# Layer norm in the first stage's last round: the order of mean and variance on TensorE

## The chip, the cores and the metric

One core of one Trainium2 chip runs the whole program. The metric is the device time of one launch in microseconds (us), the median of three runs. Engines are TensorE (PE; its weight loads are PEld), VectorE (DVE), ScalarE (ACT), GpSimd (POOL) and SyncE (SP).

## The reference, cut to what matters

Two layers act on x (8 batches, 256 tokens, 256 channels). The first layer is an LSTM, linear attention, an RNN and a 16-expert feed-forward. The second layer begins with another LSTM, whose output is normalized before its attention projects it:

```python
def _L1_attn_ref(x, Wq, bq, Wk, bk, Wv, bv, gamma, beta):
    mu = jnp.mean(x, axis=-1, keepdims=True)
    var = jnp.mean(jnp.square(x - mu), axis=-1, keepdims=True)
    xn = (x - mu) * jax.lax.rsqrt(var + LN_EPS) * gamma + beta
    ...
```

The x of this function is the output of the second layer's LSTM (`_L1_cond_ref`), 256 tokens of 8 batches. The change touches only mu and var.

## The kernel before, in words

Three stages follow one another: `pipeline_one` (first layer, the second layer's LSTM and this layer norm), `attention_two`, and `pipeline_two`. Tokens are cut into NCH = 16 chunks of C = 16 tokens (CW = 128 columns of token and batch). `pipeline_one` runs NI = 20 rounds i of 16 slots each, and then four more slots. One slot is one time step of the LSTMs; the e-LSTM (second layer) runs LAG = 4 rounds behind the a-LSTM. Each engine has its own instruction list, written out by the loop over `steps()`, and takes it strictly in that order; semaphores tie the lists together. There is no planner: the order of the calls in the loops is the order of the work.

The ring of one LSTM step is: TensorE's `lstm_step` (L584; matmuls at L596) fills the gates in PSUM, VectorE transposes them (`gate_turn`, L1036), ScalarE takes a tanh (L840), VectorE makes the cell (L1043, L1045, L1048 in `cell`), ScalarE takes its tanh (L846), VectorE makes the new state lh (`state`, first instruction L1060), and TensorE's next `lstm_step` waits for lh.

In round 19, the last, most other work has run out, and the layer norm begins beside the ring. `UNITS` lists 9 units of tokens: seven pairs of chunks (units 0 to 6, 256 columns) and two single chunks (units 7 and 8). `UNIT_AT` gives unit 0 to round 18's slot 15, units 1 to 6 to round 19's slots 0 to 5, and unit 7 to slot 7; unit 8 comes behind the loop. For unit u in its slot:

- TensorE, at the end of its slot: `norm_mean(u)` (L766, matmuls at L775), two fp32 matmuls in four records, with the unit's columns moving, into PSUM bank xy[0]. It waits for the centering of unit u-1 (`n_d`), which read that bank.
- VectorE, between `cell` and `state`: `norm_center(u)` (L1260, instruction L1263) waits for `n_mean` and subtracts the mean in place.
- ScalarE, at the end of its slot: `norm_square(u)` (L953, instruction L958) into one of two buffers, sq[u % 2], over tmp and gs.
- TensorE, one slot later: `norm_var(u)` (L779, matmuls at L787) waits for `n_sq` and makes four fp32 matmuls of one moving column, with the squares as 128x128 weights, in eight records, into bank xy[1].

Where a slot has both a `norm_var` (of unit u-1) and a `norm_mean` (of unit u), TensorE's list has them at L825 to L828, behind all its other work of the slot. That is so in slots 0 to 5 of round 19. In slot 15 of round 18 and in slot 7 there is only a mean, in slots 6 and 8 only a variance. The first root over the variances (`norm_sqrt(0)`, L960) is taken in slot 7 and wants units 0 to 6. Slots 3 and 6 also have an LSTM input projection (L453), slot 1 a product into z (L105).

Of the kernel before, what the change touches and what calls it, by code (L numbers as in the profile page):

```python
# [64 lines left out]
def attends(i):  # L65

    return 1 <= i <= NCH
# [32 lines left out]
def split_matmul(pe, out, w, x, start, last=False):  # L100

    ins = None
    for k in range(KT):
        for wp, xp in ((0, 0), (1, 0), (0, 1)):
            ins = pe.matmul(out, w[wp](k), x[xp](k), start=start, stop=last and k == KT - 1 and xp == 1,  # L105
                            skip_group_check=True)
            start = False
    return ins


def pipeline_one(nc, t, xs, hs1, x2d, late, qkv):


    with ExitStack() as ctx:
# [138 lines left out]
        def wh(n, m):  # L253

            return (lambda k: w_hi[n][:, k, m * P:(m + 1) * P], lambda k: w_lo[n][:, k, m * P:(m + 1) * P])

        def cols(hi, lo, a, b):
            return (lambda k: hi[:, k, a:b], lambda k: lo[:, k, a:b])

        def bias(n, m):  # L260
            o = NB[n][0] + m * P
            return brow[:, o:o + P]
# [198 lines left out]
        def project_c(pe):  # L461

            for m in range(KT):
                pe.matmul(g_c[:, :, m, :], bias("c_b", m), ones2[:, :], start=(m == 0), stop=False,
                          skip_group_check=True)
                last = split_matmul(pe, g_c[:, :, m, :], wh("c_wx", m), cols(x1_h, x1_l, 0, CW), False)
            return last
# [9 lines left out]
        def steps():  # L477

            return [(i, slot) for i in range(NI + 1) for slot in range(C if i < NI else E0)]

        def xn(c, n):

            return hs1[:, :, (LAG + 1 + c) * CW:(LAG + 1 + c + n) * CW]
# [15 lines left out]
        def unit_at(i, slot, lag):  # L499

            return UNIT_AT.get(i * C + slot - lag)

        def pair_at(i, slot, lag):

            return PAIR_AT.get(i * C + slot - lag)
# [77 lines left out]
        def _(pe):  # L583
            def lstm_step(i, slot):  # L584

                n = i * C + slot
                par, u = slot // QS % 2, slot % QS
                on = [(0, "a_wh")] * (i < NCH) + [(1, "e_wh")] * (n >= FIRST_STEP["e"])
                pe.wait_ge(l_hi, n)
                for w, part in ((w_hi, 0), (w_lo, 0), (w_hi, 1)):  # L590
                    if part == 1:
                        pe.wait_ge(l_lo, n)
                    for ae, name in on:
                        for k in range(KT):
                            for j in range(4):
                                last = pe.matmul(gate_block(ae, j, par), lh[:, part, ae, k, u, :],  # L596
                                                 columns(w[name], k, j), start=False, stop=(part == 1 and k == KT - 1),
                                                 skip_group_check=True, tile_position=(0, j * 32))
                last.then_inc(l_pe, 1)
# [18 lines left out]
            def rnn_step(i, slot):  # L618
                n = nth("c", i, slot, NCH * C)
                if n is None:  # L620
                    return
                s = n % C
                prev = (s - 1) % C * B
                pe.wait_ge(c_hi, n)
                pe.wait_ge(c_32, n)
                for m in range(KT):
                    for k in range(KT):
                        for wt in (w_hi, w_lo):
                            pe.matmul(g_c[:, s, m, :], wt["c_wh"][:, k, m * P:(m + 1) * P],
                                      c_hh[:, k, prev:prev + B], start=False, stop=False, skip_group_check=True)  # L630
                pe.wait_ge(c_lo, n)
                for m in range(KT):
                    for k in range(KT):
                        last = pe.matmul(g_c[:, s, m, :], w_hi["c_wh"][:, k, m * P:(m + 1) * P],
                                         c_hl[:, k, prev:prev + B], start=False, stop=(k == KT - 1),
                                         skip_group_check=True)
                last.then_inc(c_pe, 1)
# [62 lines left out]
            def w1(i, slot):  # L700

                n = nth("w1", i, slot, N_E)
                if n is None:
                    return
                for h in range(2):
                    if n > 0:
                        pe.wait_ge(g_32, 2 * n - 1 + h)
                    pe.matmul(xy[h][:, :], w1s[:, n % E1, :],
                              tst[:, n // E1 % 2, 4 * h:4 * h + 4, :].rearrange("p h n -> p (h n)"), start=True,
                              stop=True).then_inc(xy_full, 1)  # L710

            def spread(i, slot):

                n = nth("w2", i, slot, N_E)
                if n is None:
                    return
                pe.wait_ge(z_free, Z_AT[n // E1 + 2, 14] + 1)
                pe.wait_ge(gp_free, n)
                if slot == 2 and attends(i):
                    pe.wait_ge(v_read, i)  # L720
                if slot in (5, 7) and attends(i):
                    pe.wait_ge(nd_read, 2 * (i - 1) + (slot - 3) // 2)
                for k in range(KT):
                    for wt in (wt_h, wt_l):
                        last = pe.matmul(gp[:, k, :], sel[:, n % E1, k, :], wt[:, :], start=(k == 0 and wt is wt_h),
                                         stop=(wt is wt_l), skip_group_check=True)
                last.then_inc(gp_full, 1)

            def values(i, slot):

                if i > 1:
                    pe.wait_ge(nd_read, 2 * (i - 1))
                split_matmul(pe, gp[:, KT:2 * KT, :].rearrange("p k n -> p (k n)"),
                             (lambda k: ac_h[:, k, :], lambda k: ac_l[:, k, :]),
                             (lambda k: w_hi["wv"][:, k, :], lambda k: w_lo["wv"][:, k, :]), start=True,
                             last=True).then_inc(v_full, 1)
# [29 lines left out]
            def norm_mean(u):  # L766

                c, n = UNITS[u]
                pe.wait_ge(e_kept, 2 * (c + n))
                pe.wait_ge(g_32, 2 * N_E)  # L770
                pe.wait_ge(prep_set, 3)
                if u > 0:
                    pe.wait_ge(n_d, u)
                for k in range(KT):
                    last = pe.matmul(xy[0][:, 0:n * CW], mean_w[:, :], xn(c, n)[:, k, :], start=(k == 0),  # L775
                                     stop=(k == KT - 1))
                last.then_inc(n_mean, 1)
# [23 lines left out]
            for i, slot in steps():  # L801
                if (i, slot) == (LAG, E0):
                    pe.wait_ge(e_reset, 2)
                if (i, slot) == (1, 0):
                    pe.wait_ge(rest_lo, LO_MAIN)
                    pe.wait_ge(loaded_const, 16 * (len(consts) + 1))
                    pe.wait_ge(row2_sent, 16)
                elif (i, slot) == (LAG, 0):
                    pe.wait_ge(rest_lo, LO_ALL)
                lstm_step(i, slot)  # L810
                w1(i, slot)
                rnn_step(i, slot)
                misc(i, slot)
                spread(i, slot)
                if slot == 1 and attends(i):
                    values(i, slot)
                project_steps(i, slot)
                if slot in (4, 6) and attends(i):
                    sums(i, slot // 2 - 2)
                w2(i, slot)  # L820
                if slot == C0 - 1 and attends(i):
                    pe.wait_ge(x1_split, i)
                    pe.wait_ge(c_32, (i - 1) * C)
                    project_c(pe)
                if unit_at(i, slot, 1) is not None:  # L825
                    norm_var(unit_at(i, slot, 1))
                if unit_at(i, slot, 0) is not None:
                    norm_mean(unit_at(i, slot, 0))  # L828
                if pair_at(i, slot, 0) is not None:
                    norm_spread(pair_at(i, slot, 0))  # L830
            norm_mean(NPAIR)
# [1567 lines left out]
```

## Time and profile before

| | |
|---|---|
| median of 3 runs (lowest to highest) | 2730.02 us (2724.48 to 2731.41) |
| profiled execution, its own time | 2729.23 us |
| its span, first to last instruction | 2727.2 us |
| PE busy / PEld busy | 2445.4 us (90%) / 2042.8 us (75%) |
| DVE busy / ACT busy / POOL busy | 1926.5 us (71%) / 1156.3 us (42%) / 398.2 us (15%) |
| mean granted TensorE clock | 0.94 of full speed |

Busy shares are means over three stages with different limits. Times in a timeline are counted from the first instruction. A "granted clock" of 1.00 is TensorE's 2.4 GHz, 0.50 is 1.2 GHz. A matmul's end is modelled; its start and the starts and ends on DVE and ACT are recorded.

### The profile page before, as it was taken

What the parts mean: (1) busy time and instruction counts of PE and PEld (TensorE: products, weight loads), DVE (VectorE), ACT (ScalarE), POOL (GpSimd) and SP (SyncE); (2) the same over time, 40 slices, a digit from 0 to 9 for tenths busy, and PEclk for the clock granted to TensorE, in tenths of its full rate; (3) what the DMA queues carried; (4) which work ended last, traced back from release to release, by engine and by line L of the source; (5) the groups of instructions that cost most, each with busy time, mean ns of one, the idle gap of its engine ahead of it and who ended that gap; (6) DMA issues with size and microseconds to landing.
All of it is one profiled execution on the core that took longest, in us unless ns stands there. A gap on an engine that the chain in (4) does not pass through costs nothing. (4 is left out here: it accounts for less than half of the span.)

```text
span 2727.2 us, 119354 instructions
## 1 busy us (share of the span) xinstructions
PE 2445.4 (90%) x50848; PEld 2042.8 (75%) x50848; DVE 1926.5 (71%) x7414; ACT 1156.3 (42%) x3693; POOL 398.2 (15%) x412
## 2 busy tenths in 40 slices
PE   3678999999999999987768859999999999999999
PEld 1455677777777777654536648999999999999998
DVE  4757777777777777788666656677777776666774
ACT  3225555555555555556346722333333333333333
POOL 0000000000000000000019701222222222222222
PEclk9668999999999999999859958999999999999999
DMA  5000000000000000100013230000000000000000
GB/s 171 1 2 3 5 5 6 5 5 5 5 5 5 5 5 5 36 12 27 4 44 108 77 109 7 9 9 9 9 9 9 9 9 9 9 9 9 5 5 6
DMA packets 53051, 53.66 MB, mean 20 GB/s; under 512 B 24982, under 2 KB 47144, under 8 KB 50602
## 3 DMA queue, kind: packets, MB, share of 16 engines
q1 hardware_dynamic: 47318, 29.70, 4.0%
q0 software_dynamic: 1728, 12.58, 1.3%
q8 instruction: 402, 6.59, 1.0%
q10 hardware_dynamic: 3476, 3.75, 0.5%
q14 instruction: 127, 1.04, 0.1%
HBM read 39.46 MB, written 6.55 MB: 17 GB/s over the span
## 5 line engine op out<-in xcount | busy, mean ns | idle before, releaser
L105 PE MATMUL p<-xn,m_h 128*128 128x128 f16 x6144 | 559.1, 220 | 0.0
L105 PE MATMUL p<-xn,m_l 128*128 128x128 f16 x3072 | 530.3, 220 | 0.0
L105 PEld LDWEIGHTS p<-xn,m_h 128*128 128x128 f16 x6144 | 480.9, 98 | 1.8
L596 PE MATMUL lg_b<-xn,lh 128*32 128x256 f16 x6144 | 303.0, 294 | 85.5 <-DVE lh L1060 77.3
L2119 POOL TENSOR_TENSOR xn<-qkv_w,xn 128x384 f16<-128x384 f32 x256 | 234.3, 915 | 904.5 <-ACT xn L2077 904.5
L1036 DVE STREAM_TRANSPOSE gt<-lg_b 128x512 f32<-128x512 f32 x324 | 230.2, 710 | 187.1 <-PE lg_b L596 184.8
L840 ACT ACTIVATE gl<-gt 128x128 f32<-128x128 f32 x324 | 100.2, 309 | 602.8 <-DVE gt L1036 602.1
L855 ACT ACTIVATE hm<-xy,b 128x512 f32<-128x512 f32 x512 | 347.9, 680 | 0.0
L105 PEld LDWEIGHTS p<-xn,m_l 128*128 128x128 f16 x3072 | 301.1, 98 | 0.7
L2003 PE MATMUL po<-m_h,xn 128*128 128x256 f16 x1536 | 292.6, 272 | 1.9 <-DVE xn L2158 1.9
L596 PEld LDWEIGHTS lg_b<-xn,lh 128*32 128x32 f16 x6144 | 161.1, 102 | 173.3 <-DVE lh L1060 128.8
L596 PE MATMUL lg_b<-e_wh_hi,lh 128*32 128x256 f16 x4096 | 210.8, 283 | 31.3 <-DVE lh L1060 29.1
L2067 ACT ACTIVATE cand<-g_b 128x16 f32<-128x16 f32 x256 | 47.1, 184 | 385.2 <-PE g_b L1967 385.2
L2003 PE MATMUL po<-m_l,xn 128*128 128x256 f16 x768 | 208.8, 272 | 0.0
L2233 DVE SCALAR_TENSOR_TENSOR zm<-zr,cand 128x16 f32<-128x16 f32 x256 | 44.4, 173 | 204.2 <-ACT cand L2067 202.1
L762 PE MATMUL yo<-hm,w2f 128*32 128x256 f32 x2048 | 162.3, 390 | 25.1 <-DVE tmp L1086 24.8
L2077 ACT ACTIVATE xn<-qkv_w 128x384 f16<-128x384 f32 x256 | 133.9, 523 | 106.1 <-DVE qkv_w L2142 106.1
L2062 ACT ACTIVATE zr<-g_b 128x32 f32<-128x32 f32 x256 | 50.6, 198 | 270.4 <-PE g_b L1951 270.4
L1945 PEld LDWEIGHTS g_b<-xn,gxu_w 128*128 128x128 f16 x4096 | 136.5, 96 | 38.1 <-DVE xn L2238 33.1
L2227 DVE TENSOR_TENSOR rh_l<-rh,rh_h 128x16 f16<-128x16 f32 x256 | 143.5, 561 | 27.7 <-DVE rh L2223 1.4
L2003 PEld LDWEIGHTS po<-m_h,xn 128*128 128x128 f16 x1536 | 148.8, 97 | 17.5 <-issue 2.3
L1945 PE MATMUL g_b<-xn,gxu_w 128*128 128x8 f16 x4096 | 140.5, 166 | 23.0 <-DVE xn L2238 21.9
(387 smaller groups left out, 6218.2 us busy)
## 6 DMA issues: line engine op xcount, KB each, us to landing
m_stage<-in_m_w POOLq DMA_DIRECT2D x12, 1024.0 KB, 5.2
hs<-in_m_w SPq DMA_DIRECT2D x14, 384.0 KB, 3.2
x_dram<-x SPq DMA_DIRECT2D x16, 128.0 KB, 2.1
xs<-in_l_wv SPq DMA_DIRECT2D x1, 2048.0 KB
attention_dram<-att SPq DMA_DIRECT2D x16, 128.0 KB, 2.8
xn<-x_dram SPq DMA_DIRECT2D x16, 128.0 KB, 2.4
out_dram<-xn SPq DMA_DIRECT2D x16, 128.0 KB, 2.2
xn<-attention_dram SPq DMA_DIRECT2D x124, 16.0 KB, 1.7
```

The costliest lines, as they stand in the source:

```text
L105: ins = pe.matmul(out, w[wp](k), x[xp](k), start=start, stop=last and k == KT - 1 and xp == 1, skip_group_check=True)
L596: last = pe.matmul(gate_block(ae, j, par), lh[:, part, ae, k, u, :], columns(w[name], k, j), start=False, stop=(part == 1 and k == KT - 1) ...
L762: last = pe.matmul(yo[q * HD:(q + 1) * HD, :, :], w2f[:, n % E1, :], tok[:, :, q, :], start=True, stop=True, skip_group_check=True, tile_p ...
L840: act.activation(gl[:, :].rearrange("p (m b) -> p m b", b=B), gt[:, :].rearrange("p (m n) -> p m n", n=32)[:, :, slot % QS * B:(slot % QS ...
L855: act.activation(hm32[:, n % 2, h * 512:(h + 1) * 512], xy[h][:, :], ACT.Gelu, bias=b1[:, n % E1:n % E1 + 1], scale=1.0 / S).then_inc(g_32, 1)
L1036: dve.transpose(gt[:, :], lg_b[slot // QS % 2][:, :, :, :].rearrange("p g a x -> p (g a x)"))\
L1945: pe.matmul(o[:, slot % 8, m, :], w[:, k, m * P:(m + 1) * P], h(g_hh, k), start=False, stop=False, skip_group_check=True)
L2003: last = pe.matmul(po[:, half, :], x[:, n % 2, r], w[:, tl, :], start=(first and x is a_h and w is m3_h), stop=(end and x is a_l), skip_gr ...
L2062: act.activation(zr[:, :], g_b[slot // 8][:, slot % 8, 0:4].rearrange("p m b -> p (m b)"), ACT.Tanh, scale=0.5 / S).then_inc(zr_act, 1)
L2077: act.activation(a_h[:, n % 2, :], a32[:, n % 2, :], ACT.Copy).then_inc(a_hi, 1)
L2119: pool.tensor_tensor(a_l[:, n % 2, :], a32[:, n % 2, :], a_h[:, n % 2, :], ALU.subtract).then_inc(a_lo, 1)
L2227: dve.tensor_tensor(rh_l[:, :, :], rh32[:, :].rearrange(kb, b=B), rh_h[:, :, :], ALU.subtract).then_inc(rh_lo, 1)
```

## The change

In TensorE's loop `norm_mean` of a slot's unit is put ahead of `norm_var` of the unit before. No instruction is added or removed, no wait is changed, and the other engines' lists stay as they are.

```diff
@@ -822,10 +822,10 @@
                     pe.wait_ge(x1_split, i)
                     pe.wait_ge(c_32, (i - 1) * C)
                     project_c(pe)
+                if unit_at(i, slot, 0) is not None:
+                    norm_mean(unit_at(i, slot, 0))
                 if unit_at(i, slot, 1) is not None:
                     norm_var(unit_at(i, slot, 1))
-                if unit_at(i, slot, 0) is not None:
-                    norm_mean(unit_at(i, slot, 0))
                 if pair_at(i, slot, 0) is not None:
                     norm_spread(pair_at(i, slot, 0))
             norm_mean(NPAIR)
```

## Rows read from the trace of the kernel before

**Rows 1.** The page: busy time by engine, and the granted clock in 40 slices.
```profile
PE 2445.4 (90%) x50848; PEld 2042.8 (75%) x50848; DVE 1926.5 (71%) x7414; ACT 1156.3 (42%) x3693; POOL 398.2 (15%) x412
PEclk9668999999999999999859958999999999999999
```
**Rows 2.** Busy by windows: length, PE, PEld, DVE, ACT, POOL, clock, DMA, GB/s.
```profile
1302.00:1415.00 113.00, 73.99 (x934) 46.31 (x927) 72.61 (x256) 41.33 (x101) 1.17 (x4) 0.67 0.01 3
1415.00:1700.00 285.00, 229.28 (x3649) 193.42 (x3648) 173.47 (x484) 142.30 (x449) 133.87 (x68) 0.81 0.29 82
```
**Rows 3.** Waits from 1315.3 to 1347.5: total us, times, longest.
```profile
DVE hs L1263 <- PE xy L775: 6.3, 5, 2.2
```
**Rows 4.** Timeline, slot 1 of round 19: start, duration, engine, line.
```profile
1325.03 0.72 DVE L1036 STREAM_TRANSPOSE gt<-lg_b 128x512 f32<-128x512 f32 x1 [1.18 <-PE lg_b L596]
...
1326.27 1.02 PEld L787 LDWEIGHTS xy<-mean_w,gs 128*128 128x128 f32 x8
...
1326.45 0.19 DVE L1048 SCALAR_TENSOR_TENSOR cl<-pl_ 128x32 f32<-128x32 f32 x1
...
1327.24 1.11 PE L775 MATMUL xy<-hs,mean_w 128*128 128x256 f32 x4
1328.38 0.69 DVE L1263 TENSOR_TENSOR hs<-hs,xy 128x512 f32<-128x512 f32 x1 [1.74 <-PE xy L775]
1328.99 0.18 DVE L1060 SCALAR_TENSOR_TENSOR lh<-gl,tl_ 128x32 f16<-128x32 f32 x1
...
1329.23 0.12 PEld L596 LDWEIGHTS lg_b<-e_wh_hi,lh 128*32 128x32 f16 x8 [1.28 <-DVE lh L1060]
```
**Rows 5.** Timeline, slot 0.
```profile
1319.15 1.48 PEld L787 LDWEIGHTS xy<-mean_w,tmp 128*128 128x128 f32 x8 [0.21 <-issue]
...
1320.57 2.05 PE L775 MATMUL xy<-hs,mean_w 128*128 128x256 f32 x4
...
1322.66 0.69 DVE L1263 TENSOR_TENSOR hs<-hs,xy 128x512 f32<-128x512 f32 x1 [1.72 <-PE xy L775]
```
**Rows 6.** Timeline, slot 2.
```profile
1330.91 1.11 PE L775 MATMUL xy<-hs,mean_w 128*128 128x256 f32 x4
...
1332.03 0.19 DVE L1048 SCALAR_TENSOR_TENSOR cl<-pl_ 128x32 f32<-128x32 f32 x1
1332.14 0.68 DVE L1263 TENSOR_TENSOR hs<-hs,xy 128x512 f32<-128x512 f32 x1
```
**Rows 7.** Timeline, slots 3 and 4.
```profile
1338.19 0.69 DVE L1263 TENSOR_TENSOR hs<-hs,xy 128x512 f32<-128x512 f32 x1 [2.23 <-PE xy L775]
...
1339.03 0.12 PEld L596 LDWEIGHTS lg_b<-e_wh_hi,lh 128*32 128x32 f16 x8 [1.28 <-DVE lh L1060]
...
1339.93 0.72 DVE L1036 STREAM_TRANSPOSE gt<-lg_b 128x512 f32<-128x512 f32 x1 [0.51 <-PE lg_b L596]
...
1341.36 0.19 DVE L1048 SCALAR_TENSOR_TENSOR cl<-pl_ 128x32 f32<-128x32 f32 x1
...
1341.88 0.69 DVE L1263 TENSOR_TENSOR hs<-hs,xy 128x512 f32<-128x512 f32 x1 [0.33 <-PE xy L775]
```
**Rows 8.** Timeline, slot 6, where there is a variance and no mean.
```profile
1348.92 1.78 PEld L787 LDWEIGHTS xy<-mean_w,tmp 128*128 128x128 f32 x8 [0.41 <-issue]
...
1349.45 0.19 DVE L1060 SCALAR_TENSOR_TENSOR lh<-gl,tl_ 128x32 f16<-128x32 f32 x1 [0.29 <-ACT tl_ L846]
...
1350.72 0.14 PEld L596 LDWEIGHTS lg_b<-e_wh_hi,lh 128*32 128x32 f16 x8
...
1352.24 0.72 DVE L1036 STREAM_TRANSPOSE gt<-lg_b 128x512 f32<-128x512 f32 x1 [2.20 <-PE lg_b L596]
```
**Rows 9.** Windows between the changes of clock.
```profile
1319.90:1326.00 6.10, 5.22 (x43) 3.69 (x44) 2.43 (x9) 1.39 (x4) 0.00 (x0) 0.50 0.01 3
...
1336.80:1347.20 10.40, 7.75 (x104) 5.70 (x107) 5.70 (x20) 2.97 (x7) 0.24 (x1) 0.98 0.00 0
1347.80:1367.00 19.20, 14.67 (x168) 9.42 (x160) 11.14 (x44) 7.48 (x17) 0.00 (x0) 0.50 0.01 2
```

## The prediction

> **What bounds the kernel now.** I read the page first: TensorE is busy for 90% of the span, at a clock that is full but for the start and the slices around the middle [rows 1]. That share says nothing of the place that the change touches, so I cut the span by stages. The stretch from 1302 to 1415 us is the end of the first stage: of 113 us TensorE is busy for 74.0, VectorE for 72.6, and the mean clock is 0.67 [rows 2]. Nobody is full there; it is a ring of latencies. Everything behind it starts when it ends, so a microsecond taken out of the ring is one off the span, and one taken elsewhere is none.
>
> Then the list of waits for the slots concerned (slot 15 of round 18 to slot 5 of round 19). VectorE's centering, L1263, stood idle for TensorE's mean, L775, five times and 6.3 us in all [rows 3]. This wait is on the ring: the centering stands in VectorE's list ahead of the new state lh, and TensorE's next step needs lh. The timeline of slot 1 shows the chain [rows 4]. TensorE starts the variance's weight loads at 1326.27, the mean's matmuls only at 1327.24, and they end at 1328.35. VectorE had issued the cell at 1326.45 and had then nothing to do until 1328.38. The centering is followed by lh 0.61 us later (1328.99), and by TensorE's next step at 1329.23. So from the mean's end to the next step there are 0.88 us (1329.23 - 1328.35) in which TensorE idles, and in front of the mean stand 0.97 us of variance (1327.24 - 1326.27) that nobody on the ring wants.
>
> **What the change does.** Its count is zero: nothing is added, nothing removed; six times, in slots 0 to 5, eight load and matmul records of a variance go behind the four of a mean. No DMA and no other queue is passed. Two waits are moved with them. The mean's wait, for the centering of the unit before, was met a slot ago. The variance's wait, for the square of the unit before, now stands behind the mean, which makes it less often late. What is queued behind the variance is TensorE's next LSTM step.
>
> The gain per slot has three caps. First, it can't be more than VectorE's wait. Second, it can't be more than the variance that goes out of the way: 0.97 us at 2.4 GHz, and 1.42 us in slot 0 (1319.15 to 1320.57), where the clock fell on the way [rows 4, 5]. Third, the variance now lies between the mean and the next step, in the 0.88 us that centering and state take. TensorE must finish it before it takes the next step; what it ran over came off the gain. Where TensorE's queue decides, the slot goes from variance + mean + 0.88 to mean + variance: the gain is 0.88 whatever the clock is, as long as VectorE was waiting for at least that long.
>
> Slot by slot:
> - Slot 0, wait 1.72 us [rows 5]: 0.88. The next step would start right behind the variance; VectorE, which has its cell by then, is no longer last.
> - Slot 1, wait 1.74 [rows 4]: 0.88. The mean's end comes 0.97 earlier, and the variance then runs for 0.97 in a cover of 0.88, so TensorE is last by 0.09.
> - Slot 2: the mean ends at 1332.02 and the cell starts at 1332.03, so the centering at 1332.14 waited for nothing [rows 6]: 0. The order can't hurt either: TensorE is finished at the same time as before, 0.96 us ahead of where the next step may start.
> - Slot 3, wait 2.23 [rows 7]: 0.88. Here the projection is in front of both, and over 0.9 us of the wait stays.
> - Slot 4, wait 0.33 [rows 7]: VectorE's own order decides then. In slot 2 the centering starts 0.11 us behind the start of the cell (1332.03 to 1332.14) [rows 6]; here it would start at 1341.47 in place of 1341.88: 0.41.
> - Slot 5 repeats slot 4 with the same wait of 0.33, the fifth of the five in [rows 3]: 0.41.
>
> The sum is 3 x 0.88 + 2 x 0.41 = 3.46 us. The cost of moving the variance is nothing where the centering covers it. If that cover were gone it would be its 0.97 us at full clock and 1.8 at 1.2 GHz: slot 6 shows a variance that really is in the way, with lh begun at 1349.45 and the next step at 1350.72, only when its loads end [rows 8]. The same rows bound what the trace doesn't show, the hand-over from a mean to a variance and from a variance to a step: the step's load began 0.02 us behind the variance's last load (1350.70 to 1350.72), so I take it as nothing. Worst it is the 0.41 us which a first load idled behind other work in slot 6, three times in the three queue-bound slots, 1.2 us; best, loads slip under the mean's last matmul and the three slots give the whole 0.97, 0.3 us more. The sum thus lies between 2.2 and 3.8.
>
> Nothing later waits for the variance sooner: the root over units 0 to 6 is in slot 7, behind the variance of slot 6, which isn't moved. So the profiled execution would go from 2729.23 to 2725.8 us. It lies 0.8 us under the median of the three runs, so on that scale the forecast is 2726.6.
>
> **The clock.** It is the one thing that the change may move by more than its own sum. It stood at 1.2 GHz from 1319.9 to 1326.0, at 2.4 through slots 4 and 5, and at 1.2 again from 1347.8 to 1367 [rows 9]. TensorE had its idle gap in each of the full slots and kept the clock for 10.4 us with 7.75 busy. The change takes idle time out of five slots and no work.
>
> The Trainium skill (TensorE: Matmul & The Clock Gate, section "Why this matters for your kernels") asks for dense work with no idle gaps to hold the higher level. By that rule the change also buys clock, which is the second case below; this trace is only half on its side, since the clock that held in 10.4 us with 7.75 busy was gone behind them [rows 9].
>
> **The rivals.**
> - The clock holds into slots 6 to 8. Those are at 1.2 GHz now. A step from its first load to the transpose takes 1.52 us there (1350.72 to 1352.24) and 0.90 at full clock (1339.03 to 1339.93) [rows 7, 8]: 0.62 for each of three slots, and in slot 6 the variance would end before lh and free another 1.03 (1350.72 less 1349.69, which is lh's start plus the 0.24 from lh to a step). That is 2.9 us, so 2723.7. For it: less idling. Against it: that fall came right behind slots 4 and 5, in which the change saves only 0.41 us of idling each.
> - The other side: the clock falls earlier, so that slots 4 and 5, full now, run at half. Then a step costs 0.62 more, and mean and variance together take 3.6 us in place of 1.8 (twice slot 6's 1.8, one for each as they are about alike) from 0.1 us ahead of the transpose. The next step starts 3.5 behind the transpose, where by VectorE alone it would be 2.4 (1.54 to the centering, 0.61 and 0.24). Each slot loses 0.6 + 1.1 = 1.7. Two such slots and half a one in slot 3 lose 4.3, against 3.5 won: slower by 0.8, so 2730.8. It decides from two lost slots on. For it: the clock was down twice here [rows 9] beside waits of at most 2.2 us [rows 3]. Against it: no pause gets longer.
> - The change does nothing: the hand-overs between fp32 loads eat what the mean wins, the wait on the mean becomes one on TensorE's queue, and the next step starts where it did. 2730.0. Against it is the 0.02 us of slot 6; for it, only that no slot of before has a variance behind a mean.
>
> **How the numbers follow.** The forecast, 2726.6, gets 0.62, the held clock 0.15, the earlier fall 0.12, nothing 0.11. A measurement of this kernel can tell about 0.3% from no change, 8.2 us; every case lies within that. What is left is the scatter: three runs of the same kernel lie 7 us apart, and the attention stage runs at a mean clock of 0.81 over 285 us [rows 2], which a shift may disturb either way. The range takes the cases from 2723.7 to 2730.8 and 3 to 5 us beyond: 2719 to 2734. Faster by over 0.3% (under 2721.8) I give 0.09, mostly from the held clock; slower by as much 0.03; within 0.3% 0.88.
>
> **What would show it.** In slots 0 to 5 the mean's matmuls start where the variance's loads did. L1263's wait for L775 falls from 6.3 us to about 2 (0.8 left in slot 1, some 1.2 in slot 3, near none in 0, 4 and 5). Slots 4 and 5 last 0.41 us less from transpose to transpose. In slots 0 and 1 TensorE's next step starts right behind the variance's last load, without the 0.88 of idling. The first stage ends some 3.5 us earlier, and nothing before slot 0 moves. The prediction is wrong if that wait stays at 6 us, if the slots don't shorten where it falls, or if the changes of clock move and carry more than the wait.

## The result and the profile after

The changed kernel takes 2716.51 us (median of 8 runs, 2714.97 to 2722.57) against 2725.39 (8 runs, 2721.86 to 2731.88): a ratio of 0.9962, with a 95% interval of 0.9949 to 0.9975. That is 8.9 us in place of the forecast 3.4 (2730.02 less 2726.6), and 2716.51 lies below the range. On another chip it was 2718.07 against 2730.41, ratio 0.9951 [0.9935, 0.9966]; one run of before there took 7198.22 us and is left out of all medians and ranges here. The profiled execution takes 2716.23 us, its span 2714.4.

The page of the changed kernel, answering to [rows 1]: TensorE's busy time falls by 12.6 us without one instruction less. The same matmuls ran at a higher clock, but only 4.2 us of this fall lie in the slots that the change touches; 7.6 lie ahead of them and 0.9 behind.
```profile
PE 2432.8 (90%) x50848; PEld 2038.1 (75%) x50848; DVE 1925.9 (71%) x7414; ACT 1154.7 (43%) x3693; POOL 397.5 (15%) x412
PEclk9678999999999999999869859999999999999999
```
The waits of the same slots (1309.3 to 1336.4 here), answering to [rows 3]:
```profile
DVE hs L1263 <- PE xy L775: 1.6, 3, 1.3
```
The wait that was to go has gone from 6.3 to 1.6 us, near the 2 that was expected, though not where: 1.26 are left in slot 1 and 0.20 in slot 3, where 0.8 and 1.2 were expected. Slot 1's timeline, answering to [rows 4]:
```profile
1318.01 0.72 DVE L1036 STREAM_TRANSPOSE gt<-lg_b 128x512 f32<-128x512 f32 x1 [1.72 <-PE lg_b L596]
...
1319.36 1.48 PE L775 MATMUL xy<-hs,mean_w 128*128 128x256 f32 x4
1319.43 0.19 DVE L1048 SCALAR_TENSOR_TENSOR cl<-pl_ 128x32 f32<-128x32 f32 x1
...
1320.46 1.08 PEld L787 LDWEIGHTS xy<-mean_w,gs 128*128 128x128 f32 x8
...
1320.88 0.69 DVE L1263 TENSOR_TENSOR hs<-hs,xy 128x512 f32<-128x512 f32 x1 [1.26 <-PE xy L775]
1321.48 0.18 DVE L1060 SCALAR_TENSOR_TENSOR lh<-gl,tl_ 128x32 f16<-128x32 f32 x1
...
1321.72 0.12 PEld L596 LDWEIGHTS lg_b<-e_wh_hi,lh 128*32 128x32 f16 x8 [0.18 <-DVE lh L1060]
```
The mean comes first, and the variance's eight loads (1320.46, 1.08 us) lie where TensorE had idled; the next step's load waits 0.18 us for lh in place of 1.28. The prediction had TensorE last here by 0.09 us, and it isn't. Slot 0, answering to [rows 5], shows the other case: at 1.2 GHz the variance ends behind lh, and the step's load (1316.49) starts only when the variance's loads end (1314.43 + 2.04).
```profile
1314.43 2.04 PEld L787 LDWEIGHTS xy<-mean_w,tmp 128*128 128x128 f32 x8
...
1315.10 0.69 DVE L1263 TENSOR_TENSOR hs<-hs,xy 128x512 f32<-128x512 f32 x1 [0.16 <-PE xy L775]
1315.70 0.18 DVE L1060 SCALAR_TENSOR_TENSOR lh<-gl,tl_ 128x32 f16<-128x32 f32 x1
...
1316.49 0.14 PEld L596 LDWEIGHTS lg_b<-e_wh_hi,lh 128*32 128x32 f16 x8
```
Slots 3 and 4, answering to [rows 7]: 0.20 us of slot 3's 2.23 are left, and slot 4's centering starts 0.10 us behind the cell.
```profile
1328.17 0.69 DVE L1263 TENSOR_TENSOR hs<-hs,xy 128x512 f32<-128x512 f32 x1 [0.20 <-PE xy L775]
...
1329.92 0.72 DVE L1036 STREAM_TRANSPOSE gt<-lg_b 128x512 f32<-128x512 f32 x1 [0.51 <-PE lg_b L596]
...
1331.34 0.19 DVE L1048 SCALAR_TENSOR_TENSOR cl<-pl_ 128x32 f32<-128x32 f32 x1
1331.44 0.68 DVE L1263 TENSOR_TENSOR hs<-hs,xy 128x512 f32<-128x512 f32 x1
```
**Where the 12.8 us between the two profiled executions went.** I measured each profile by VectorE's transposes, one per LSTM step, in three parts: up to the transpose of round 18's slot 15; the "stretch" of eight steps from there to round 19's slot 7, which holds every slot that the change touches; and what lies behind. The first part (1315.56 and 1309.55 us) is 6.0 us shorter in the changed kernel, though no instruction in it differs. The stretch takes 36.68 and 29.92 us, 6.8 less. The rest is equal within 0.1. The stretch's own row for the changed kernel (length, PE, PEld, DVE, ACT, POOL, clock, DMA, GB/s):
```profile
1309.55:1339.47 29.92, 25.37 (x347) 20.73 (x348) 19.68 (x70) 8.72 (x23) 0.58 (x2) 0.89 0.02 7
```
Its mean clock is 0.89; in the kernel before it was 0.79 by the same view. So three questions were open: whether the 6.0 us ahead belong to the change, what the order is worth at one clock, and what moved the clock.

### The profile page after: what moved, and what is told of

Its sections match the earlier page's. It is cut to its first block and busy times, and to the rows that moved or that the text cites. A ratio compares the mean times of both kernels' runs of the same rounds, so it can differ in the third digit from the quotient of the medians.

```text
span 2714.4 us, 119354 instructions
## 1 busy us (share of the span) xinstructions
PE 2432.8 (90%) x50848; PEld 2038.1 (75%) x50848; DVE 1925.9 (71%) x7414; ACT 1154.7 (43%) x3693; POOL 397.5 (15%) x412
```

## The experiments

Each row has one profile, which shows the clock in one execution. "Stretch" is as above; "low" is the time in it at 1.2 GHz. Ratios are against the kernel before on the same chip; its medians on the five other chips were 2727.9 to 2730.4 us.

| kernel | median us (lowest to highest, runs) | ratio [95%] | stretch | low |
|---|---|---|---|---|
| before, first profile | 2725.39 (2721.86 to 2731.88, 8) | | 36.68 | 15.7 |
| b_null: before again | 2729.55 (2720.43 to 2734.72, 12) | 0.9991 [0.9978, 1.0004] | 46.34 | 41.0 |
| b_p1: before again | 2729.01 (1) | | 43.06 | 32.2 |
| b_p2: before again | 2722.02 (1) | | 36.68 | 15.7 |
| after, first profile | 2716.51 (2714.97 to 2722.57, 8) | 0.9962 [0.9949, 0.9975] | 29.92 | 6.8 |
| a_again: changed again | 2718.07 (2714.57 to 2719.13, 6) | 0.9951 [0.9935, 0.9966] | 27.42 | 0 |
| a_p1: changed again | 2716.22 (1) | | 29.92 | 6.8 |
| a_again2: changed again | 2716.96 (2713.78 to 2718.48, 6) | 0.9962 [0.9948, 0.9977] | 27.40 | 0 |
| b_fill: before, 2 extra matmuls a slot | 2718.88 (2715.37 to 2721.55, 6) | 0.9955 [0.9939, 0.9971] | 30.40 | 0 |
| b_fill1: before, 1 extra a slot | 2718.40 (2717.60 to 2722.32, 10) | 0.9968 [0.9958, 0.9977] | 30.39 | 0 |
| a_fill: changed, 2 extra a slot | 2717.53 (2714.60 to 2719.91, 6) | 0.9954 [0.9938, 0.9969] | 27.70 | 0 |
| b_filltail: before, extra to stage end | 2718.09 (2714.67 to 2721.80, 12) | 0.9962 [0.9950, 0.9975] | 30.40 | 0 |
| a_filltail: changed, extra to stage end | 2717.44 (2714.80 to 2721.07, 12) | 0.9957 [0.9945, 0.9969] | 27.69 | 0 |
| s01: swapped in slots 0, 1 | 2724.28 (2716.20 to 2733.37, 12) | 0.9988 [0.9970, 1.0006] | 29.15 | 0 |
| s345: swapped in slots 3, 4, 5 | 2718.73 (2716.53 to 2724.86, 12) | 0.9967 [0.9953, 0.9980] | 36.89 | 20.5 |
| s12345: swapped in slots 1 to 5 | 2720.72 (2716.21 to 2721.28, 6) | 0.9964 [0.9951, 0.9976] | 30.53 | 6.8 |
| b_fill15: before, 4 extra in slot 15 | 2726.18 (2718.42 to 2737.01, 12) | 0.9990 [0.9975, 1.0004] | 46.40 | 41.4 |
| a_idle: changed, VectorE delay | 2717.99 (2715.34 to 2724.59, 10) | 0.9964 [0.9948, 0.9980] | 29.43 | 0 |
| a_novar2: changed, variances left out (output wrong) | 2715.65 (2714.11 to 2720.33, 6) | 0.9961 [0.9946, 0.9976] | 27.40 | 0 |
| b_split: half of each variance ahead | 2715.97 (2710.40 to 2732.45, 12) | 0.9960 [0.9947, 0.9974] | 42.20 | 38.2 |

**1. Both kernels again, and both with the clock held up.** The edit of b_fill and a_fill puts matmuls with unused results at the end of TensorE's work in slot 15 and slots 0 to 6, in the order of before and in the changed one:
```diff
+            def fill(k):
+                if k not in FILL:                # FILL = {k: 2 for k in range(8)}
+                    return
+                pe.wait_ge(gp_free, N_E)
+                for _ in range(FILL[k]):
+                    pe.matmul(gp[:, :, :].rearrange("p k n -> p (k n)"), w_hi["c_wh"][:, 0, 0:P],
+                              w_hi["c_wx"][:, :, :].rearrange("p k n -> p (k n)"), start=True, stop=True, ...)
...
                     norm_spread(pair_at(i, slot, 0))
+                fill(i * C + slot - NORM)
```


> The kernel before once more, unchanged. It measures the scatter and gives a second look at where the clock falls. Theory A (the order's own gain is 3 to 3.5 us, and the rest of the difference is TensorE clock: part of it brought by the order, part by chance in places the change doesn't touch): no difference beyond 0.15% (4 us) in the medians, but the times of the first mean in the two profiles may differ by some us. From the transpose of round 18's slot 15 to that of round 19's slot 7 it takes 36.7 us in the profile of before; another profile may show 33 to 37, by where the clock falls. Rival B (the whole difference comes from the order alone and each profile repeats): 36.7 within 0.3, and the first mean within 1 us of 1315.4.

> The changed kernel once more. Theory A: 6 to 10 us under before by the medians; from slot 15's transpose to slot 7's 28 to 32 us (29.9 in the first profile), with slots 4 and 5 again 0.41 shorter each than before. Rival B: the same 29.9 within 0.3, and the first mean 6 us earlier than in every profile of before, which would say that something ahead of the changed slots has changed.

> The order of before, with two extra fp16 matmuls (128x128 weights, 512 columns, results unused, about 0.43 us at full clock) behind TensorE's work of slot 15 and slots 0 to 6 of the last rounds; they fit into the 0.88 us in which TensorE idled there. Theory A (the clock falls for TensorE's idling): the clock stays up through these slots, and from slot 15's transpose to slot 7's it takes 31 to 33 us in place of 36.7, so about 4 us faster than before without the change of order. Rival B (clock has nothing to do with it): within 0.5 us of before, or slower by up to 3 us as the extra matmuls stand in the way.

> The changed order with the same extra matmuls. Theory A: the stretch from slot 15's transpose to slot 7's takes 28 to 29.5 us, 3 to 3.5 less than the same extra matmuls in the order of before: the order's own gain at one clock. About 1 us faster than the changed kernel, as its one low stretch of 6.9 us at slot 0 goes too. Rival B: the difference between the two orders with the extra matmuls is the same 6.8 us as without them, and this kernel is no faster than the changed one.

Measured: the kernel before gives the same median, but its second profile is quite another: the stretch takes 46.34 us, nearly all of it at 1.2 GHz.
```profile
1309.84:1356.18 46.34, 39.35 (x347) 28.27 (x348) 20.03 (x71) 8.73 (x23) 0.58 (x2) 0.56 0.01 4
```
Its slot 15 transpose is at 1309.84, against 1315.56 in the first profile and 1309.55 in the changed kernel. So the 6 us ahead of the stretch are chance. Over all four profiles of each kernel the mean of that time is 1310.8 and 1310.9; the means of the stretch are 40.7 and 28.7. The stretch carries the whole difference.

The changed kernel again, with no low clock in the stretch:
```profile
1312.74:1340.16 27.42, 22.23 (x347) 18.13 (x348) 19.59 (x71) 8.73 (x23) 0.59 (x2) 1.00 0.02 7
```
With extra matmuls in the order of before, and then in the changed order:
```profile
1310.70:1341.10 30.40, 26.35 (x363) 18.60 (x364) 19.86 (x71) 8.72 (x23) 0.58 (x2) 1.00 0.02 6
```
```profile
1309.21:1336.91 27.70, 25.69 (x363) 18.80 (x364) 19.58 (x70) 8.71 (x23) 0.58 (x2) 1.00 0.02 7
```
This is the main finding. More work on TensorE made the kernel before 11.5 us faster (2718.88 against 2730.41), with its order untouched. In its profile the clock stayed at 2.4 GHz, and the stretch is 10.3 us under the mean of before. And at one clock the two orders lie 2.70 us apart. The extra matmuls cost the changed order 0.28 (27.70 against 27.42), so its own gain is 3.0. Theory A held in kind, but its sizes were off. It looked for 33 to 37 us in b_null (46.34), 28 to 32 in a_again (27.42), 31 to 33 and 4 us gained in b_fill (30.40 and 11.5), and 28 to 29.5 in a_fill (27.70), which is no faster than the changed kernel beyond the scatter.

**2. The swap in part of the slots, and extra matmuls to the end of the stage.** The swap is bound to `i == NI - 1 and slot in (0, 1)`, or `(3, 4, 5)`. In the other two FILL runs on with five a slot, three where there is a spread matmul.

> The mean goes ahead of the variance in slots 0 and 1 alone. With extra matmuls in both orders the order's own gain at full clock was 2.70 us (30.40 less 27.70 from slot 15's transpose to slot 7's), of which slots 0 and 1 had 0.36 and 0.90. Theory A1 (the clock is lost or kept by the idling around slots 15, 0 and 1, and a low stretch begun there feeds on itself): 1.3 us of the order's own, and most of the 7 to 9 us of clock: 8 to 10 us under before. Theory A2 (every slot's idling adds its share to the chance of a fall): 1.3 plus about a third of the clock: 3 to 5 us under before, and slots 3 to 6 are still found at the low clock in the profile or in the scatter of the times, which stays at 10 us or more.

> The mean goes ahead of the variance in slots 3, 4 and 5 alone; the order's own gain there at full clock was 0.62, 0.41 and 0.42, 1.45 us. Theory A1: the low stretch of slots 0 and 1 stays and may run on: 1.5 to 4 us under before. Theory A2: 1.5 plus half of the clock or more: 5 to 7 us under before.

> The order of before with extra matmuls (results unused) to the end of the first stage: two a slot up to round 19's slot 6, then five a slot, three where the slot has a spread matmul. In every profile so far the clock is low for some 50 us behind slot 6 or 7 and the 12 steps behind slot 7's transpose take 49.9 us. Theory A (the idling brings the low clock): these 12 steps take 43 to 46 us, and the kernel is 15 to 19 us under before. Rival (the extra matmuls hold up the steps, or the clock falls for another reason): 49 us or more, 9 to 12 us under before as with the extra matmuls in the first slots alone.

> The changed order with the same extra matmuls to the end of the stage. Theory A: 2.7 us less than the order of before with them from slot 15's transpose to slot 7's, and 2 to 3.5 us less by the medians: what the order is worth when the clock is taken out. The fastest kernel of this study, 17 to 21 us under before. Rival (the order's whole effect was the clock): the two with extra matmuls are within 1 us.

Measured: A1 fails. The swap in slots 0 and 1 left the times spread from 2716 to 2733 us, and its interval reaches 1; that in slots 3 to 5 gave 9.5 us though its profile has a low stretch of 20.5 us from slot 0 on. That low stretch ended in slot 3, the first swapped one (the clock is back 25.2 us behind slot 15's transpose), where the order of before stayed low into slot 6 in two of four profiles. A2 fits s01 (3 to 5 us under before was 3.9, with a scatter of 17) and is too small for s345 (5 to 7 was 9.5).
```profile
1312.59:1349.48 36.89, 30.84 (x347) 22.99 (x348) 19.88 (x71) 8.73 (x23) 0.58 (x2) 0.72 0.02 5
```
The profiles at full clock throughout also size the order slot by slot, from transpose to transpose: slot 0 3.61 (b_fill1) to 3.25, slot 1 4.91 to 4.02, slot 2 3.25 both, slot 3 4.45 (s01) to 3.55, slot 4 3.68 to 3.26, slot 5 3.67 to 3.26. That is 0.36 + 0.89 + 0 + 0.90 + 0.42 + 0.41 = 2.98 us.

Behind slot 7 the extra matmuls did not pay: the 12 steps took 51.84 and 50.01 us where they take 48.7 to 49.95 in all others, and neither kernel came to the 15 to 21 us under before that theory A gave them (10.1 and 10.8). The clock was up for longer parts, but the matmuls stood in front of steps, as the rival had it. The two orders differ by 2.71 us in the stretch; the medians by 0.65, which a scatter of 6 us can't tell from either.

**3. The idling put back, and more profiles.** a_idle adds one product to VectorE's part of slots 0 to 5:
```diff
+                if i == NI - 1 and slot < 6:
+                    dve.tensor_tensor(dmx[:, :, :], rcd[:, :, :], att[:, :, :], ALU.mult)
                 if slot == E0 and i > LAG:
```


> The changed order, with one extra VectorE product (128x256 fp32, result unused, about 0.4 us) between the centering and the state in slots 0 to 5: each step waits 0.4 us longer and TensorE idles as long as it did before the change. Direct cost at full clock: 6 x 0.4 = 2.4 us or less, as slots 1 and 3 are bound by TensorE's queue, so about 1.5 to 2.4. Theory A (less idling on TensorE is what keeps the clock): more than the direct cost is lost; in part of the executions the slots fall to the low clock again, the times scatter over 10 us or more as before the change, and the median is 4 to 8 us above the changed kernel. Rival C (it is the order itself, variance behind mean, that keeps the clock, whatever the idling): 1.5 to 2.4 us above the changed kernel, with its narrow scatter of 5 us.

> The kernel before, one more look at where the clock falls. So far slot 15's transpose to slot 7's took 36.7 and 46.3 us. Theory A: between 31 (clock kept throughout, which the filled order of before shows at 30.4) and 46.5 (low throughout), and not the same as both others.

> The kernel before, again one look: between 31 and 46.5 us. The mean over the four looks at this order should be 8 to 12 us above the mean of the looks at the changed order (29.9 and 27.4 so far), if this stretch alone makes the difference of the medians.

> The changed kernel, a third look: 27.4 to 31 us from slot 15's transpose to slot 7's, whatever the phase of the clock. If one look shows it low throughout (over 38 us), the change doesn't protect from the low clock and the theory of a self-sustaining low stretch falls.

Measured: the stretch is 29.43 us, 2.0 more than the changed kernel at full clock, as the direct cost was worked out. The clock stayed up in the profile and the median is that of the changed kernel; three of ten runs lie at 2721.7 to 2724.6, where one of the changed kernel's 21 is above 2720. TensorE idles for 5.0 us of slots 0 to 5, against 5.4 in the kernel before and 3.0 in the changed one at full clock. So pauses of nearly the old sum did not bring the loss back, which speaks against theory A in its plain form (less idling keeps the clock); rival C is nearer. Whether the three slower runs had a low stretch isn't shown. The other profiles came out as expected: 43.06 and 36.68 before, 29.92 changed.

**4. What in the order keeps the clock.** a_novar2 skips the variances of units 0 to 5 and fills their columns with one small matmul (`if u < 6: pe.sem_inc(n_var, 1); return`), b_split calls `norm_var` for the unit's first chunk ahead of `norm_mean` and for the second behind it. b_fill1 has `FILL = {k: 1 for k in range(8)}`.

> The changed kernel again, beside the next three. 2716 to 2719 us, with a scatter of 5 us or little more; from slot 15's transpose to slot 7's 27 to 30 us.

> The changed kernel without the variance matmuls of units 0 to 5 (their variances are a constant here, so the output is wrong): nothing stands between the mean and the next step, at either clock. Theory D (what keeps a low stretch going is idling at the low clock; in the changed order a variance of 1.8 us at 1.2 GHz covers the 0.88 us in which VectorE works, so TensorE doesn't idle there and the clock comes back; in the order of before it idles 0.88 us in every slot at any clock): taking this work away brings the idling back. The kernel is not faster than the changed one, though it has 48 matmul records less: 0 to 5 us slower, with a scatter of 8 us or more, and low slots of about 4.4 us in the profile where a full one takes 3.3. Rival E (less work on TensorE's queue is simply faster, the clock follows chance): 0.5 to 1.5 us faster than the changed kernel, with its scatter.

> Half of each variance (the unit's first chunk) stays ahead of the mean, half goes behind it, in slots 0 to 5. At full clock the centering then waits 0.47 us less in slots 0, 1 and 3 and 0.33 to 0.41 less in 4 and 5; at 1.2 GHz the half behind the mean takes 0.9 us and covers the 0.88. Theory D: no idling at the low clock, so low stretches end as in the changed kernel: 6 to 10 us under before, within 2 us of the changed kernel, scatter 5 to 8 us. Rival E: half of the order's own gain, 1 to 2 us under before, with the scatter of before.

> The order of before with one extra matmul a slot in place of two (about 0.2 us at full clock, 0.43 at 1.2 GHz; result unused), slot 15 to slot 6. It leaves some 0.45 us idle per slot at the low clock where two left nearly none. Theory D: in between, 3 to 9 us under before, and low stretches of several slots are still met in some executions, so a scatter of 8 us or more. Rival E: within 1 us of before.

Measured: theory D falls at both ends. With the variances left out there is nothing to cover VectorE's 0.88 us, and no low clock came in its profile; the stretch takes exactly as long as with them.
```profile
1311.32:1338.72 27.40, 17.65 (x301) 12.21 (x302) 19.57 (x71) 8.73 (x23) 0.58 (x2) 1.00 0.02 7
```
Rival E wanted 0.5 to 1.5 us off and got 1.3 in the median, none of it from the stretch. That also shows that the variance behind the mean costs nothing at full clock. With the variances split, most runs are fast (ten of twelve at 2710 to 2720 us), but two took 2730 and 2732, a scatter of 22 us where theory D gave 5 to 8, and the profile of the slowest has the clock low for 38 of 42 us:
```profile
1313.09:1355.29 42.20, 39.09 (x347) 30.40 (x347) 20.02 (x71) 8.72 (x23) 0.58 (x2) 0.55 0.02 5
```
In its low slots TensorE is hardly ever idle; this is slot 4 (its L1066 is L1060 of before, the new state):
```profile
1340.05 1.01 PE L787 MATMUL xy<-mean_w,tmp 128*128 128x1 f32 x4
...
1340.92 2.05 PE L775 MATMUL xy<-hs,mean_w 128*128 128x256 f32 x4
...
1342.77 0.85 PE L787 MATMUL xy<-mean_w,tmp 128*128 128x1 f32 x4
...
1343.86 0.62 PE L596 MATMUL lg_b<-e_wh_hi,lh 128*32 128x256 f16 x8 [0.24 <-DVE lh L1066]
```
Its idle time is 0.24 us of 5.2, and the clock stayed low all the same. One extra matmul a slot did about as much as two: 2718.40 us with a scatter of 4.7, where theory D wanted 8 or more and rival E no gain.

**5. Where the low clock starts.** s12345 keeps the variance first in slot 0 alone; b_fill15 has `FILL = {0: 4}`.

> The mean goes ahead of the variance in slots 1 to 5, and not in slot 0. In the profiles so far the clock fell 3.7 to 4.7 us behind slot 15's transpose in all six kernels with the variance first in slot 0, in two of seven with the mean first there, and in none of five with extra matmuls in slot 15. Theory F (the fall is decided in slots 15 and 0, by TensorE's pause in slot 15 and what stands first in slot 0; how long the low stretch lasts is decided by the order in the slots behind): the profile has the fall 4 us behind slot 15's transpose, and the median lies 2 to 4 us above the changed kernel's, 6 to 9 us under before. Rival G (the slots behind decide alone): within 1 us of the changed kernel.

> The order of before, with four extra matmuls in slot 15 alone (0.9 us in the 1.7 us pause behind the mean of unit 0, results unused). Theory F: no fall in slot 0 in the profile; slots 3 to 5 can still fall, as with the mean ahead in slots 0 and 1 alone (2724.3 us against 2728.2 before, 2716 to 2733). So 3 to 7 us under before, in two groups of times. Rival G: no more than 2 us under before.

Measured: s12345 fell 4.1 us behind slot 15's transpose, as theory F says, and was back 6.8 us later. Its median lies 3.8 us above a_again2's, its ratio of 0.9964 within the changed kernel's own intervals, so F and G stay undivided by the times. b_fill15 speaks against F: with the pause of slot 15 filled the clock still fell, 5.0 us behind the transpose, and stayed low through all the slots of before's order; its times (2.0 us under before) are those of rival G.
```profile
1309.98:1356.38 46.40, 40.28 (x351) 28.47 (x351) 20.03 (x70) 8.72 (x23) 0.58 (x2) 0.55 0.02 4
```

One half of F may stand. Of the 15 profiles without extra matmuls in slots 0 to 6, the clock fell 3.7 to 5.0 us behind slot 15's transpose in all eight with the variance first in slot 0, and in two of the seven with the mean first there. Thirteen of the 15 were the ground on which F was made, so this is a count and not a test of it. What is behind that fall differs too. The three low stretches that were followed by the mean first in slots 1 to 5 (after, a_p1, s12345) all ended after 6.8 us, and no other came before slot 7. Of the seven with a variance, or half of one, first in slot 1, each ran on for 20 us or more or was followed by a second one.

## Why the prediction was wrong, point by point

**The sum of the order was nearly right.** It said 3.46 us and the runs show 2.98 at full clock. Slots 1 to 5 are as forecast: 0.88, 0, 0.88, 0.41, 0.41 against 0.89, 0, 0.90, 0.42, 0.41. The cover for the variance and VectorE's own order in slots 4 and 5 held. In slots 1 and 3 the number is partly luck. TensorE is not last at full clock either, as a_again's slot 1 shows:
```profile
1320.44 1.08 PE L775 MATMUL xy<-hs,mean_w 128*128 128x256 f32 x4
...
1321.14 1.08 PEld L787 LDWEIGHTS xy<-mean_w,gs 128*128 128x128 f32 x8
...
1322.40 0.12 PEld L596 LDWEIGHTS lg_b<-e_wh_hi,lh 128*32 128x32 f16 x8 [0.18 <-DVE lh L1060]
```
The variance's loads begin 0.38 us before the mean ends (1321.52) and are over at 1322.22, so the step waits for lh. The gain is what left the front of the mean: the centering's wait goes from 1.07 (b_fill1) to 0.18 us in slot 1, and from 1.09 (s01) to 0.20 in slot 3. The 2.23 that was read for slot 3 [rows 7] held clock as well. Slot 0 was mis-sized, 0.88 against 0.36. Its wait of 1.72 us [rows 5] was taken as the order's, but the clock had fallen in it. With that fall in both kernels slot 0 takes 5.69 and 4.68 us, 1.01 less; at full clock the centering waits only 0.27 us there, as b_fill's timeline shows (its L1275 is L1263):
```profile
1316.35 0.69 DVE L1275 TENSOR_TENSOR hs<-hs,xy 128x512 f32<-128x512 f32 x1 [0.27 <-PE xy L776]
```

**The term that failed is the clock's.** The sum took the low time inside the changed slots as given, that is, it put the clock's share of the gain at nothing. That low time was 15.7 us in the stretch of the very profile that I read, and a part of it, inside slots 2 and 3, isn't named in the prediction (length, PE, PEld, DVE, ACT, POOL, clock, DMA, GB/s):
```profile
1333.00:1336.40 3.40, 3.40 (x56) 2.58 (x56) 1.42 (x6) 1.02 (x3) 0.00 (x0) 0.53 0.02 5
```
Its one case with a gain by clock, "The clock holds into slots 6 to 8", at 2.9 us and 0.15, was right in its kind and for one slot in its size. In the two first profiles slot 6 goes from 4.70 us (1347.54 to 1352.24) to 3.04, 1.66 less, where this case gave it 0.62 + 1.03. But the clock fell again 1.2 us behind slot 7's transpose, and slots 7 and 8 gave nothing.
```profile
1336.43 0.72 DVE L1036 STREAM_TRANSPOSE gt<-lg_b 128x512 f32<-128x512 f32 x1 [0.55 <-PE lg_b L596]
...
1339.47 0.72 DVE L1036 STREAM_TRANSPOSE gt<-lg_b 128x512 f32<-128x512 f32 x1 [0.55 <-PE lg_b L596]
```
The prediction's own last sign of being wrong, that changes of clock carry more than the wait, is what came.

By b_fill1 the order of before takes 30.39 us at full clock; the four profiles of it average 40.7. So the low clock cost the kernel before 10.3 us in these eight steps, 6.3 of them in the profile that I read (36.68 less 30.39). The changed order loses 1.2 (28.7 less 27.4). Of the 12.0 us that the stretch shrank in the mean, 3.0 are the order and 9.0 the clock. Behind the stretch 0.9 us are given back in the mean of the profiles (1374.9 and 1375.8), which leaves 11.2 against the 9 to 12 of the medians.

**The range failed with it,** and not by the effect alone. Of the 10.1 us between 2726.6 and 2716.51, 5.5 are the effect (8.9 in place of 3.4). The other 4.6 are the base: three runs of before gave 2730.02, and the eight have 2725.39. From that base a range of the same width would have held the result; from the 2730.41 of the second chip it would not have held that chip's 2718.07. The sum also took one execution as the kernel. The profiles of before have a stretch of 36.7 to 46.3 us, so the one that it read has the shortest, and the three times of before, 7 us apart, were a hint. That scatter was read as noise beside the change. The change removed much of it: 2716 to 2741 us over 126 runs of before (standard deviation 4.3), 2714 to 2723 over the changed kernel's 21 (2.0).

**The slower rival** priced a low slot at 1.7 us more in the changed order. The order of before pays more: slot 4 takes 6.07 us low and 3.68 full. These are its weight loads in b_null's slot 4:
```profile
1340.50 1.78 PEld L787 LDWEIGHTS xy<-mean_w,tmp 128*128 128x128 f32 x8 [0.41 <-issue]
1342.16 1.40 PEld L775 LDWEIGHTS xy<-hs,mean_w 128*128 128x128 f32 x4
```
Both the variance and the mean take nearly twice as long, and both are in front of the centering. In the changed order only the mean is. What slots 4 and 5 would cost at the low clock in that order isn't shown, since no profile has it.

**The Trainium skill's advice** (TensorE: Matmul & The Clock Gate, section "Why this matters for your kernels") to keep the matmuls dense pointed the right way: the case that it stood beside came true in slot 6, and filling the pauses recovered 11 us in the old order. The pauses that its table warns of are longer than any in these eight steps, the longest of which is the 1.7 us in slot 15. As a rule for which slot falls it did not serve: a_novar2 and a_idle idle more than the changed kernel (7.7 and 5.0 us of slots 0 to 5, against 3.0) and kept the clock in their profiles, b_split at 1.2 GHz idles 1.4 us there and did not.

**Open.** What sends the clock down in slots 0 to 3, and what lets a low stretch last 7 us in one execution and 41 in the next of the same program, isn't settled. Shown are: extra matmuls in all eight steps work, in slot 15 alone they don't; pauses at the low clock are not needed to keep it low (b_split). That the order in slots 3 to 5 decides more than that in slots 0 and 1 is only suggested: s345 and s01 lie 5.5 us apart, but their intervals overlap. No run varied the kind of product that stands first, so whether it is the variance's one-column products, rather than the order, that go with a low clock is untested. One profile per kernel can't give the chances of each.

## What to carry to other kernels

Put the product that another engine waits for ahead of one that nobody waits for, and look for a cover for the latter: here the variance became free at full clock. Before summing waits, split them by granted clock. A wait read in a 1.2 GHz stretch holds clock as well as order, and a change that touches TensorE's list may return the clock's share too. Take several profiles of the kernel before where its times scatter by more than the change is worth.

## What the runs showed of the hardware

Adding 16 matmuls of unused results to eight steps made the program 11 us faster (b_fill), and 8 did about as much (b_fill1, ratio 0.9968). The same program, in the same eight steps, ran 41 us at 1.2 GHz in one execution and 15.7 in two others; TensorE was busy for 39.35 of the 46.34 us of the slow one.
